# Three exponentials for eight bases, merged root chains and runs of 32 columns in the window layer of a four-layer kernel

## The reference

```python
def _fastkan(x, ln_g, ln_b, ws, wb, bb):
    ln = _layernorm(x, ln_g, ln_b)
    basis = jnp.exp(-((ln[..., None] - GRID) / DENOM) ** 2)      # 8 bases, GRID = linspace(-2, 2, 8), DENOM = 4/7
    flat = basis.reshape(*basis.shape[:-2], -1)
    return flat @ ws.T + jax.nn.silu(x) @ wb.T + bb

y = _layernorm(wins, pn_g, pn_b)                  # 8x8 windows, norm over the 32 channels        (PN)
a = y.reshape(b, WS, WS, c, S).transpose(0, 2, 3, 1, 4).reshape(b, WS * c, WS * S)
a = _fastkan(a, ...k1...)                         # norm over 8 rows x 2 channels                 (K1)
d = y.reshape(b, WS, WS, c, S).transpose(0, 1, 3, 2, 4).reshape(b, WS * c, WS * S)
d = _fastkan(d, ...k2...)                         # norm over 8 columns x 2 channels              (K2)
e = _fastkan(y, ...k3...)                         # norm over the 32 channels                     (K3)
z = _fastkan(a + d + e, ...k4...)                 #                                               (K4)
out = z + wins
```

## Time and profile before

| what | value |
|---|---|
| three runs | 12029.0, 12041.97 (median), 12056.08 us |
| the profiled execution | 12020.56 us, span from first to last instruction 12018.7 us |
| mean granted TensorE clock | 0.927 |
| TensorE / its weight loads | 9492.6 / 4623.4 us busy (79% / 38%) |
| VectorE | 9408.9 us (78%) |
| ScalarE | 8396.4 us (70%) |
| GpSimd | 298.0 us (2%) |

### The profile page before, as it was taken

How to read it: one execution, slowest core, us unless ns; L and a number is a source line. 1 busy time by engine, 2 the same in 40 slices (tenths; PEclk the granted TensorE clock), 3 DMA queues, 4 the chain that set the end, 5 groups by cost and what they waited for, 6 DMA issues and landing times. The chain is left out here.

```text
span 12018.7 us, 360844 instructions
## 1 busy us (share of the span) xinstructions
PE 9492.6 (79%) x152226; PEld 4623.4 (38%) x152226; DVE 9408.9 (78%) x10971; ACT 8396.4 (70%) x5579; POOL 298.0 (2%) x132
## 2 busy tenths in 40 slices
PE   0888778885657799868888888888888888887787
PEld 0333223333435666533333333333333333333444
DVE  6677656657776666579999999999999999998776
ACT  0555455555531133279999999999999999998777
POOL 0000000000004500000000000000000000000000
PEclk9999999997879899989999999999999999998899
DMA  7888788886642244355555555555555555554555
GB/s 265 236 239 239 208 228 246 244 229 243 269 195 64 69 153 153 127 100 105 104 102 108 102 106 104 107 102 105 102 109 101 107 101 107 104 107 75 178 176 162
DMA packets 1165596, 1796.78 MB, mean 149 GB/s; under 512 B 124832, under 2 KB 929824, under 8 KB 1094048
## 3 DMA queue, kind: packets, MB, share of 16 engines
q1 hardware_dynamic: 1164320, 1777.49, 58.1%
HBM read 701.15 MB, written 402.65 MB: 92 GB/s over the span
## 5 line engine op out<-in xcount | busy, mean ns | idle before, releaser
L1886 DVE SCALAR_TENSOR_TENSOR grown_ex<-ratio,ex 128x2048 f32<-128x2048 f32 x1024 | 2330.8, 2286 | 250.9 <-PE out L2019 107.4
L2019 PE MATMUL out<-ex,kan_basis 32*32 32x512 f32 x32768 | 1451.1, 654 | 637.8 <-DVE z L1868 359.6
L1764 ACT ACTIVATE ex<-ex 128x2048 f32<-128x2048 f32 x1024 | 1925.8, 1899 | 4.1
L2019 PE MATMUL out<-grown_ex,kan_basis 32*32 32x512 f32 x32768 | 1563.8, 645 | 51.7 <-DVE grown_ex L1886 50.8
L547 PE MATMUL conv<-uc,w 128*32 128x512 f32 x12288 | 1442.8, 611 | 21.0 <-DMA uc<-u 21.0
L1760 ACT ACTIVATE ex<-kin,offset 128x2048 f32<-128x2048 f32 x512 | 1013.2, 1991 | 68.8 <-PE out L2019 60.5
L456 ACT ACTIVATE v<-conv,cb 128x512 f32<-128x512 f32 x512 | 350.5, 684 | 789.8 <-PE conv L547 786.4
L2019 PEld LDWEIGHTS out<-ex,kan_basis 32*32 32x32 f32 x32768 | 396.6, 107 | 1113.5 <-issue 1045.1
L2019 PEld LDWEIGHTS out<-grown_ex,kan_basis 32*32 32x32 f32 x32768 | 541.3, 107 | 673.5 <-issue 582.4
L2138 DVE TENSOR_TENSOR d<-xt 128x2313 f32<-128x2313 f32 (+2 forms) x256 | 622.1, 2494 | 215.3 <-PE acc L2195 215.0
L2195 PE MATMUL acc<-d,weights 32*32 32x512 f32 x16384 | 667.1, 632 | 113.3 <-issue 109.6
(11 more groups left out here) (284 smaller groups left out, 17527.2 us busy)
## 6 DMA issues: line engine op xcount, KB each, us to landing
uc<-u SPq DMA_DIRECT2D x2048, 129.0 KB, 2.8
xt<-in_x SPq DMA_DIRECT2D x128, 1024.0 KB, 7.3
t<-v SPq DMA_DIRECT2D x128, 1024.0 KB, 5.8
back_k<-ku SPq DMA_DIRECT2D x1024, 128.0 KB
xt<-in_x SPq DMA_DIRECT2D x32, 2048.0 KB, 7.8
xt<-t SPq DMA_DIRECT2D x64, 1024.0 KB, 7.6
tt<-t SPq DMA_DIRECT2D x64, 1024.0 KB, 10.8
x<-x SPq DMA_DIRECT2D x64, 1024.0 KB, 4.9
```

The source lines that it names most:

```text
L1764: a.activation(ex[:, j], ex[:, j], ACT.Exp, scale=-1.0).then_inc(exps, 1)
L1886: v.scalar_tensor_tensor(grown_ex[:, j % 2], ratio[:], LARGEST, ex[:, j], ALU.min, ALU.mult).then_inc(grown, 1)
L2019: last = m.matmul(out[rows(i), g, :], k["kan_basis"][rows(g), kind - 1, n, :], base[rows(g), cols(i)], start=(n == 0), stop=(n == BASES - ...
```

## The change

- `ANCHORS` and `GROWTHS`: K1, K2 and K3 compute bases 0, 3 and 6 by Square and exp, and bases 1, 2, 4, 5, 7 by growths, 2 from 1 and 5 from 4; K4 keeps four anchors (0, 2, 4, 6) and four growths. Constants folded into `kan_basis` follow.
- `CHAINS`: one root chain serves K1, K2 and K3 together, another PN and K4 (of two different tiles), each over 2 or 3 x 128 columns. `q` then holds the result and there is one `q` per chain.
- `MOVED_BY_ACT`: K1 and K2 are moved by ScalarE too.
- A row of 256 columns is kept as 8 runs of 32, one for each column within a window: `columns_apart` reads x so in the centre product of PN, and `raster` reads back in the centre and silu products of K4. `turn_y`, `turn_u` and `total` then handle runs of 32.
- K3's bias is folded into two bias columns of K1's evacuation, which becomes two instructions of half the size; `total` is a plain sum.
- `c_center` holds 32x32 blocks.
- All positions are new.

```diff
-MOVED_BY_ACT = (PN,)
+MOVED_BY_ACT = (PN, K1, K2)
...
+ANCHORS = {K1: (0, 3, 6), K2: (0, 3, 6), K3: (0, 3, 6), K4: (0, 2, 4, 6)}
+GROWTHS = {kind: tuple(n for n in range(BASES) if n not in ANCHORS[kind]) for kind in KANS}
+CHAINS = ((K1, K2, K3), (PN, K4))
 UNITS = 128
...
+CENTER = {PN: 14, K1: 84, K2: 102, K3: 114, K4: 299}
+MOVE = {PN: 20, K1: 87, K2: 110, K3: 122, K4: 306}
+SQUARE = {PN: 23, K1: 90, K2: 123, K3: 132, K4: 311}
+VARIANCE = {PN: 36, K1: 100, K2: 125, K3: 136, K4: 314}
+TAKE = {PN: 39, K1: 101, K2: 127, K3: 135, K4: 316}
+SPREAD = {PN: 68, K1: 144, K2: 153, K3: 205, K4: 344}
+SCALE = {PN: 70, K1: 146, K2: 165, K3: 207, K4: 351}
+RATIO = {K1: 163, K2: 197, K3: 224, K4: 390}
+EVACUATE = {K1: 201, K2: 233, K3: 273, K4: 430}
+CHAIN = {PN: 61, K1: 136, K2: 136, K3: 136, K4: 317}
+GROW = {K1: {1: 166, 2: 176, 4: 184, 5: 187, 7: 196},
+        K2: {1: 200, 2: 203, 4: 212, 5: 218, 7: 222},
+        K3: {1: 230, 2: 236, 4: 239, 5: 245, 7: 252},
+        K4: {1: 398, 3: 404, 5: 407, 7: 410}}
+ANCHOR = {K1: (153, 155, 175),
+          K2: (176, 191, 202),
+          K3: (210, 217, 234),
+          K4: (367, 377, 393, 396)}
+EXP = {K1: (159, 172, 189),
+          K2: (192, 194, 205),
+          K3: (214, 227, 246),
+          K4: (378, 380, 397, 398)}
+PRODUCT = {K1: (172, 174, 179, 185, 190, 195, 197, 199),
+          K2: (200, 207, 209, 211, 215, 223, 225, 227),
+          K3: (231, 233, 239, 241, 246, 258, 262, 265),
+          K4: (401, 402, 408, 410, 413, 419, 424, 426)}
+TANH, SILU = {PN: 80, K4: 301}, {PN: 96, K4: 303}
+TURN_Y, TURN_U, MEASURE = 86, 123, 496
+LOAD_X, LOAD_R, STORE = 2, 396, 437
+FEED_Y, FEED_U, BACK = {K1: 55, K2: 88}, {K1: 174, K2: 182}, {K1: 219, K2: 236}
...
+        def raster(tile_):
+            return tile_.rearrange("p (r x w) -> p r w x", x=BAND, w=QUAD)
+
+        def columns_apart(tile_):
+            return tile_.rearrange("p (r w x) -> p r x w", x=BAND, w=QUAD)
...
+                if kind == K1:
+                    for odd in range(2):
+                        of_groups = [tile_.rearrange("p (i o n) -> p o i n", o=2, n=COLS)[:, odd] for tile_ in (dst, out_flat)]
+                        last = a.activation(of_groups[0], of_groups[1], ACT.Identity, bias=k["end_k1"][:, odd:odd + 1])
...
             def columns_first(tile_):
-                return tile_.rearrange("p (x rw) -> p x rw", x=BAND)
+                return tile_.rearrange("p (x r w) -> p r x w", x=BAND, w=QUAD)
 
             def rows_first(tile_):
-                return tile_.rearrange("p (rw x) -> p x rw", x=BAND)
+                return tile_.rearrange("p (r x w) -> p r x w", x=BAND, w=QUAD)
...
-            def chain(kind, t, h):
+            def chain(group, due):
+                some = slice(group.index(due[0]), group.index(due[-1]) + 1)
                 v.drain()
-                last = chain_order.before(kind, t)
-                if last is not None:
-                    dve.wait_ge(spread_ready[last[0]], last[1] + 1)
-                rsqrt_polynomial(v, y[:], q[:], t_[:]).then_inc(factors[kind], 1)
+                rsqrt_polynomial(v, y[:, 0:len(due)], q[group][:, some], t_[:, 0:len(due)], q[group][:, some]).then_inc(factors[group], 1)
...
-                v.scalar_tensor_tensor(rows_first(Z[:]), rows_first(out_flat), out_b(K3, h), columns_first(D[:]), ALU.add,
-                                       ALU.add).then_inc(summed, 1)
+                v.tensor_tensor(rows_first(Z[:]), rows_first(out_flat), columns_first(D[:]), ALU.add).then_inc(summed, 1)
...
-                            last = m.matmul(norm[rows(g), n, :], k["pn_center"][rows(n), h, rows(g)], src[rows(n), cols(g)],
+                            last = m.matmul(norm[rows(g), n, :], k["pn_center"][rows(n), h, rows(g)], columns_apart(src[rows(n), cols(g)]),
...
+                            piece = src[rows(g), cols(n)]
+                            last = m.matmul(norm[rows(n), g, :], k["c_center"][rows(g), which, :], raster(piece) if kind == K4 else piece,
...
-                        m.matmul(out[:, i, :], k["kan_silu"][:, kind - 1, :], silu_of(kind, h)[:, cols(i)], start=False, stop=False)
+                        piece = silu_of(kind, h)[:, cols(i)]
+                        m.matmul(out[:, i, :], k["kan_silu"][:, kind - 1, :], raster(piece) if kind == K4 else piece, start=False, stop=False)
```

More of the change, by code:

```diff
@@ L129, in rsqrt_polynomial @@
     dve.drain()
-    last = dve.scalar_tensor_tensor(y, q, RSQRT[0], y, ALU.add, ALU.mult)
+    last = dve.scalar_tensor_tensor(y if out is None else out, q, RSQRT[0], y, ALU.add, ALU.mult)
     dve.drain()
@@ L1460, in _ @@
             pe.wait_ge(loaded, 16 * count)
-            nc.tensor.matmul(shift[:], k["c_center"][:, 0, :], bias, start=True, stop=True).then_inc(shifted, 1)
+            for n in range(GROUP):
+                rows = slice(QUAD * n, QUAD * n + QUAD)
+                last = nc.tensor.matmul(shift[rows, :], k["c_center"][rows, 0, :], bias[rows, :], start=True, stop=True,
+                                        tile_position=(QUAD * n, QUAD * n))
+            last.then_inc(shifted, 1)
         @block.vector
@@ L1488, in _ @@
                 v.tensor_scalar(k["ratio_b"][:, n:n + 1], vec[:, 3 + 3 * n:4 + 3 * n], 2.0, None, ALU.mult)
-            for j in range(1, BASES, 2):
-                v.tensor_scalar(k["kan_basis"][:, :, j, :], k["kan_basis"][:, :, j, :], float(np.exp(BASES - 2.0 * j)), None, ALU.mult)
+            for kind in KANS:
+                for j in GROWTHS[kind]:
+                    below = max(n for n in ANCHORS[kind] if n < j)
+                    grown_by = float(np.exp(sum(BASES - 2.0 * n for n in range(below + 1, j + 1))))
+                    v.tensor_scalar(k["kan_basis"][:, kind - 1, j, :], k["kan_basis"][:, kind - 1, j, :], grown_by, None, ALU.mult)
             v.tensor_scalar(k["kan_silu"][:], k["kan_silu"][:], 0.5, None, ALU.mult)
@@ L1559, in before, with __init__, __call__ @@
         return last, t + (at - self.middle)
+class Count:
+    def __init__(self, order, each):
+        self.order, self.each, self.all = order, each, sum(each.values())
+    def __call__(self, kind, t):
+        if isinstance(t, int):
+            return sum(self.each[n] for n, _ in self.order.items[:self.order.index[kind, t]])
+        return t * self.all + (self(kind, self.order.middle) - self.all * self.order.middle)
 def window_layer(net, k, source, bias, target, stats):
@@ L1631, in exps_done, with slots_before, group_of @@
         def exps_done(kind, t):
-            return PAIRS * slot_no(kind, t) + PAIRS
+            return exps_before(kind, t) + len(ANCHORS[kind])
+        def slots_before(kind, t):
+            item = slot_no.before(kind, t)
+            while item is not None:
+                yield item
+                item = slot_no.before(*item)
+        def group_of(kind):
+            return next(group for group in CHAINS if kind in group)
+        def raster(tile_):
+            return tile_.rearrange("p (r x w) -> p r w x", x=BAND, w=QUAD)
+        def columns_apart(tile_):
+            return tile_.rearrange("p (r w x) -> p r x w", x=BAND, w=QUAD)
         class Round:
@@ L1793, in round_ @@
                             growth(kind, t, h)
-                        for j in range(PAIRS):
+                        for j in range(len(ANCHORS[kind])):
                             t, h = now.due(u, ANCHOR[kind][j])
@@ L1903, in round_ @@
                             take(kind, t, h)
-                        t, h = now.due(u, CHAIN[kind])
-                        if t is not None:
-                            chain(kind, t, h)
                         t, h = now.due(u, SCALE[kind])
@@ L1909, in round_ @@
                             scale(kind, t, h)
+                    for group in CHAINS:
+                        due = [kind for kind in group if now.due(u, CHAIN[kind])[0] is not None]
+                        if due:
+                            chain(group, due)
                     for position, step in ((TURN_Y, turn_y), (TURN_U, turn_u), (MEASURE, measure)):
@@ L1914, in round_ @@
                     for kind in KANS:
-                        for j in range(PAIRS):
-                            t, h = now.due(u, GROW[kind][j])
+                        for n in GROWTHS[kind]:
+                            t, h = now.due(u, GROW[kind][n])
                             if t is not None:
-                                grow(kind, j, t, h)
+                                grow(kind, n, t, h)
             rounds(dve, round_)
@@ L2333, in kan_arrays @@
         silu.append(u.reshape(P, P))
+    for half in a["L2_conv_k3_bb"].reshape(2, 16):
+        vec.append(np.repeat(half, 8))
     return {"kan_vec": np.stack(vec, axis=1), "kan_basis": np.stack(basis, axis=1), "kan_silu": np.stack(silu, axis=1)}
```

125 lines of the change are left out of this document (62 added, 63 removed).

## The result

The changed kernel takes 12,414.5 us, median of 4 runs (12,398.4 to 12,431.4); the kernel before, in the same comparison, 12,043.5 (12,029.0 to 12,056.1). The ratio is 1.0309 [1.0288, 1.0329]: 3.1% slower, where 0.9% faster was forecast, and 244 us above the upper end of the range. The profiled execution's span is 12,400.3 us against 12,018.7.

A forecast was written before the change was run, and what follows sets the result against it. VectorE bounds before (88.5 of 91.95 us a tile); after, a ring through ScalarE: 87.3, 89.5 with jumps, plus 0.6 for the silu, 90.1. Saving 1.85 x 63 = 117, plus 3 once, gives 11,928; range 11,680 to 12,170.

The forecast's parts named there:

- The sums: Work per tile after the change: VectorE 81.5 us, from 88.5, and ScalarE 79.5, from 86.7.
- Growths 3, 5, 7 of K4, `scale K2`, K1's growth 1, `take PN`: 24.8: Stretch of VectorE's walked order, counted from `take K3`: these steps follow without a stated wait, to 24.8 us.
- The silu's stride: K4's silu product reading in steps of 32 words: factor 1.6, +2.1 us, of which 0.6 a tile counts.
- 2.0 and 0.6 are free there: Behind K4's product 4: slack in us for the tanh of the next z and the variance of PN.
- rival of the strided silu: K4's silu product slower than bounded, delaying VectorE beyond 2.0 us of slack; 12,210 at factor 3; chance 0.22.
- the two signs that were named: Time of K4's silu products in the profile after: 0.6 us if the stride is free, over 1.4 if not.
- The jump: Where the loop jumps, every second tile: TensorE loses 4.1 us, `take K3` comes 5.9 later, ScalarE runs ahead.
- The part of the chains: VectorE's root chains, merged into one over three norms and one over two: 9.1 us for 15.8, -6.7.
- The part of the exponentials: Three anchors and three exps fewer: ScalarE -11.1 us a tile; VectorE gains three growths, +6.6, and +0.7.
- signs of being wrong: VectorE idle before `silu K4` or `move K4` (the silu), or before `scale` of K2 or PN (a wait taken as covered).
- The full sum: Rival: the ring has unseen slack, so VectorE bounds again at 84.9 us a tile, about 11,600; chance 0.12.
- Hand-overs and jumps: Rival: 0.25 us at each of some twelve hand-overs, clock drops at more places; 12,040 to 12,100; chance 0.16.

The follow-up runs named there:

- e1: Changed kernel with K4's silu product reading with unit stride: 12,187.2 us, ratio 1.0124 to the kernel before.
- e10: Changed kernel with K4's silu product issued right behind product 5, with its own semaphore for tanh: 12,369.4 us, ratio 1.0282 to the kernel before.
- e17: Changed kernel with all positions raised by 56, so only the loop's jump falls elsewhere, ahead of K2's first product: 12,206.3 us, ratio 1.0150.
- both mends: Changed kernel with `total` writing K4's input in raster order and all positions raised by 56 to move the jump: 12,018.6 us, ratio 0.9995.
- e6: Kernel before with a loop body of four tiles instead of two: 11,946.7 us, ratio 0.9930.
- e12: Order, exponentials and single chains of the kernel before, with runs of 32, `total` writing in raster order and a four-tile body: 11,901.2 us, ratio 0.9899.
- e18: e12 with a loop body of eight tiles instead of four: 11,841.0 us, ratio 0.9840 to the kernel before.
- e7: Changed kernel with a loop body of four tiles instead of two: 12,451.6 us, ratio 1.0345 to the kernel before.

## Why the prediction was wrong

- **The sums** (VectorE 81.5, ScalarE 79.5) stand. At 98.00 us a tile the busy shares 0.797 and 0.811 give 78 (without the gaps between the chains' passes, which my sum has) and 79.5. Counts, growths, exps, `total`, turns (1.22 us) and chains are as forecast. They don't set the time.
- **The step that failed first** is "Growths 3, 5, 7 of K4, `scale K2`, K1's growth 1, `take PN`: 24.8". It let K1's growth 1 start when VectorE was free. The code of `grow` waits until the product that read the same buffer last is done; that is K4's product 5, and it stands behind residual and silu products. The wait is 5.23 us in the tile shown, so `take PN` starts at 30.1 and not at 24.8. Without the stride 1.8 to 2.4 us of it are left (e1), so the step was wrong by the order alone, and the stride made the wait more than twice as long. e10 shows that taking this wait away by itself frees only 0.32 us a tile: what was missed is the whole stretch of TensorE behind it.
- **The silu's stride** was mis-sized (factor 2.0, not 1.6: 3.5 us, not 2.1) and, worse, misplaced: "2.0 and 0.6 are free there" was false, since the stretch of TensorE had no slack at all. I took 0.6 a tile; it measures 3.46 (e1). My rival of the strided silu gave it 2.0 us of slack too and decided only at 2.3. The measured factor lies under that, and the rival's mechanism held all the same. The record of 1051 ns lies between the two signs that were named, 0.6 and over 1.4 us.
- **The jump.** "With 4.1 of jump" was 7.0, and "ScalarE meanwhile runs ahead" was wrong: ScalarE's third anchor of K4 needs the `ex` slot of K3's product 6, behind the jump. The forecast had 4.3 us between the two kinds of tile; from `take K3` to the next it is 94.4 and 103.3. Moving the jump gives 2.81 a tile (e17).
- **What is left.** 98.00 - 90.1 = 7.9 us a tile were missed, 498 us. With both mends 5.82 are back, and `total` there costs 1.59 more than in the forecast: 7.4 in all. But the mends also take out what the forecast had for the two, 0.6 for the stride and up to 2.2 for the jump (89.5 - 87.3). So by estimate 4.6 to 6.8 of the 7.9 are these two, and 1.1 to 3.3 stay open.
- **The part of the chains** was about right (6.7 us of VectorE worked out, 5.99 a tile measured, with the clock's share in it unknown). The part of the exponentials wasn't tested by itself in the new order, and stays open.
- **The signs.** VectorE does wait before the take of K3, above all every second tile, as forecast. The other wait, before K1's growth 1, is at none of the places named as signs of being wrong.
- **The other rivals.** Slower had 0.28, all of it with the silu or the hand-overs. The full sum didn't come near. Hand-overs and jumps had the right sign and half the right place, but blamed 0.25 us at each hand-over, which nothing here shows, instead of one long stop.

The Trainium skill, Advanced Engine Details and Errata, section Memory Cachelines, asks for two hits on a 16-byte line for full speed; the runs agree that steps beyond such a line are slower, and none has steps short enough to test the two hits. Steps of 32 words took 1.74 times as long a record (1051 ns for 605) and 2.0 times a group, steps of 8 words 1.8 a record (1086 for 597). The Vector Engine (DVE) Microarchitecture Reference of the Trainium skill, section Measured stream behaviour on trn2, has 2.50 ns for 1.05, a factor of 2.4, for steps of 24 words on VectorE; here TensorE shows 2.0, and VectorE 1.7 (3.88 for 2.29).

## What to carry to other kernels

When an order is walked, follow each buffer that an instruction writes back to its last reader, not only the data it reads: the wait that decided this case was on a buffer of two. A busy share of 80% on every engine doesn't mean slack; ask for the longest stretch in which one engine runs without a break and another waits for its end, and keep the strided operand and the loop's jump out of that stretch. Time moved off a loaded engine pays only if the new order doesn't spend it on a ring, and the cheapest gain may be beside the change: a longer loop body gave the kernel before 0.7% with nothing else touched.

## What was unexpected of the hardware

- The loop's jump costs by its place. In the kernel before it is 4.3 us at each in e6 and, between e12 and e18, which keep its order, 30 us for 7 jumps fewer. In the changed kernel TensorE's stop is 7.0 us, and moving the jump by itself gave 208 us, while halving their number gave nothing (e7).
- TensorE also stops for issue once where there is no jump, 3.19 us in the tiles shown. Behind the variance of K3 it shows in no interval (95.3 and 95.7 us in the first tiles with it, 95.7 and 95.6 in those without); inside that variance VectorE's take waits 5.39 us (e7). What causes it is open.
- ScalarE's write in steps of 8 words takes 4.03 us for 1.97, a factor of 2.0.
- A layer that no edit touched took 785 to 872 us from its first to its last difference (842 in the kernel before, 808 in the changed one, 866 in e7, 785 in e17), so that differences under 50 us are read from the period and not from the time. Why is open.
